# Cross-attention core: the output projection of a tile as one block of twelve matmuls, or as three pieces of four

## The reference

```python
q = (x @ Wq).reshape(b, n, 32, 16)
k, v = jnp.split(ctx @ Wkv, 2, axis=-1)          # 32 heads of 16 each
q = apply_axial_rope(q, pos_map)
k = apply_axial_rope(k, ctx_pos_map)
w = jax.nn.softmax(jnp.einsum('bqhd,bkhd->bhqk', q, k) * scale, axis=-1)
attn = jnp.einsum('bhqk,bkhd->bqhd', w, v).reshape(b, n, 512)
return attn @ Wout + bout                        # x = x + this
```

## Time and profile before

| | us |
|---|---|
| time, median of 3 runs | 2159.01 |
| lowest and highest run | 2152.72 and 2161.05 |
| the profiled execution | 2174.66 |
| its span, first to last instruction | 2172.9 |
| cross core in that span, about | 587 to 1010 |
| mean granted TensorE clock | 0.958 |

### The profile page before, as it was taken

One profiled execution on the slowest core, in us unless ns is written; L12 is line 12 of the kernel. 1 busy time (PEld: TensorE's weight loads), 2 busy tenths in 40 slices (PEclk: granted clock), 3 DMA queues, 4 the chain that ended last, 5 costly groups with the idle time before them and its releaser, 6 DMA issues. The chain is left out here.

```text
span 2172.9 us, 31103 instructions
## 1 busy us (share of the span) xinstructions
PE 2018.2 (93%) x10519; PEld 1340.0 (62%) x10519; DVE 1214.0 (56%) x2649; ACT 873.1 (40%) x1535; POOL 697.4 (32%) x610
## 2 busy tenths in 40 slices
PE   7998999978799999997998899979999998999998
PEld 6875666666433334334776566657878787565664
DVE  6555766566799898875886666644323153222221
ACT  3424444355377676773443444434222221111111
POOL 0003665346423232322664755601000000232332
PEclk9998998989899999997998899989999999999999
DMA  5637676356754646444466767452112055233331
GB/s 199 222 138 187 159 158 140 104 185 250 255 145 118 152 105 154 100 127 128 173 222 205 166 162 160 121 213 105 54 44 78 1 218 208 45 60 60 66 61 36
DMA packets 150832, 297.64 MB, mean 137 GB/s; under 512 B 24594, under 2 KB 43156, under 8 KB 149588
## 3 DMA queue, kind: packets, MB, share of 16 engines
q1 hardware_dynamic: 112900, 242.29, 37.6%
q10 hardware_dynamic: 29040, 34.74, 6.2%
q0 software_dynamic: 8736, 18.62, 4.6%
HBM read 181.55 MB, written 102.50 MB: 131 GB/s over the span
## 5 line engine op out<-in xcount | busy, mean ns | idle before, releaser
L1353 ACT ACTIVATE cross_c_prob<-bank 128x512 f32<-128x512 f32 x512 | 271.1, 598 | 118.9 <-PE bank L1200 117.6
L1402 DVE TENSOR_REDUCE row_max<-bank 128x2 f32<-128x1024 f32 x248 | 290.7, 1213 | 24.6 <-PE bank L1162 23.6
L1860 PE MATMUL bank<-moe_hT,moe_w 128*128 128x512 f32 x1056 | 250.6, 393 | 7.7 <-DVE moe_w L2103 7.7
L1200 PE MATMUL bank<-stack 56*128 56x512 f32 (+4 forms) x768 | 225.7, 437 | 11.9 <-DMA stack<-first_c_max_rows 3.9
L1860 PEld LDWEIGHTS bank<-moe_hT,moe_w 128*128 128x128 f32 x1056 | 199.4, 190 | 50.1 <-issue 7.9
L1162 PE MATMUL bank<-stack 48*128 48x512 f32 (+4 forms) x720 | 184.9, 441 | 26.0 <-PEq L71 13.6
L1200 PEld LDWEIGHTS bank<-stack 56*128 56x128 f32 (+1 forms) x768 | 114.9, 197 | 142.8 <-ACT cross_c_prob L1353 68.5
L1948 PE MATMUL bank<-moe_w_e,moe_hT_e 128*128 x624 | 194.2, 465 | 6.2 <-DMA moe_w_e<-in_experts_packed 5.9
L1948 PEld LDWEIGHTS bank<-moe_w_e,moe_hT_e 128*128 128x128 f32 x624 | 116.4, 191 | 67.3 <-issue 9.6
L1162 PEld LDWEIGHTS bank<-stack 48*128 48x128 f32 (+1 forms) x720 | 92.0, 196 | 101.4 <-DVE row_max L1402 46.1
L1398 DVE CUSTOM_DVE_ANT_0 first_c_masked<-bank,later 128x128 f32<-128x128 f32 (+3 forms) x240 | 110.2, 486 | 75.9 <-PE bank L1162 73.5
(11 more groups left out here) (391 smaller groups left out, 3987.5 us busy)
## 6 DMA issues: line engine op xcount, KB each, us to landing
moe_w_e<-in_experts_packed SPq DMA_DIRECT2D x8, 2176.0 KB, 8.9
qk_parts<-first_p_parts SPq DMA_DIRECT2D x32, 512.0 KB, 2.6
stack<-qk_parts SPq DMA_DIRECT2D x64, 256.0 KB, 7.1
qk_parts<-cross_p_parts SPq DMA_DIRECT2D x32, 512.0 KB, 2.7
stack<-qk_parts SPq DMA_DIRECT2D x256, 64.0 KB, 2.6
qk_parts<-rotary_p_parts SPq DMA_DIRECT2D x32, 512.0 KB, 2.7
moe_raw<-in_shared_packed SPq DMA_DIRECT2D x11, 768.0 KB, 8.4
stack<-qk_parts SPq DMA_DIRECT2D x16, 512.0 KB, 6.3
```

The lines of the kernel that those rows point to most:

```text
L1200: last = nc.tensor.matmul(tiles[:, h], k_stack[slot][r : r + ALL_ROWS, at, m * P : (m + 1) * P], q_stack[slot][r : r + ALL_ROWS, at, q0:S] ...
L1353: nc.scalar.activation(probability(g, m, j), psum[bank_at["score", n]][:, 0:S], ACT.Exp).then_inc(s.exp_done, 1)
L1402: nc.vector.tensor_reduce(row_max[:, g % 2, m, j - 1 : j + 1], c.banks[:, first : first + WIDE, :], AX_X, ALU.max).then_inc(s.max_done, 1)
L1860: last = nc.tensor.matmul(psum[bank][:], weights(pa, f, k), hT[p % 2][:, pb, k, :], start=m == 0, stop=m == len(steps) - 1)
```

## The change

The projection of a tile is issued in three pieces of four matmuls: behind the value blocks of steps 11 and 15 of group `1 + m` and of step 3 of group `2 + m`. `add_residual` follows in DVE's order two steps behind the last piece, at step 5 of group `2 + m`. For the causal cores nothing is different.

```diff
-        THIRDS = 1 if cross else 3
-        OUT_AT = ([[(1 + m, 7)] for m in range(TT)] if cross else
+        THIRDS, RESIDUAL_LAG = 3, 2 if cross else 0
+        OUT_AT = ([[(1 + m, 11), (1 + m, 15), (2 + m, 3)] for m in range(TT)] if cross else
                   [[(1 + m // 2, step) for step in ((12, 14, 15) if m % 2 else (6, 7, 10))] for m in range(TT)])
@@
         def projected_at(g, step):
 
-            if g >= G:
+            if g >= G and step >= 0:
                 for m, thirds in enumerate(OUT_AT):
@@
-                            projected = projected_at(g, step)
+                            projected = projected_at(g, step - RESIDUAL_LAG)
                             if projected and projected[2] == THIRDS - 1:
                                 add_residual(projected[0], projected[1])
```

## The result

The changed kernel takes 2203.96 us (median of 4 runs, 2195.7 to 2210.68), the kernel before 2160.03 in the same comparison (4 runs, 2152.72 to 2167.13). The ratio is 1.0188, 95% interval 1.0166 to 1.0210: slower, by 41 us by the ratio and 44 by the medians; whether by more or less than 2% the interval leaves open. The profiled execution has 2195.7 us and a span of 2194.0.

A forecast was written before the change was run, and what follows sets the result against it. Bounds: PE and ACT waiting for each other in a ring, and DVE equally in quiet groups. Added 1.54 + 1.54 + 2.52 = 5.60 us less 3.58 removed, +2.02 a tile, +24.3 over 12 tiles: 2184 us, range 2168 to 2202.

The forecast's parts named there:

- The block's removal: Projecting groups: the block of twelve matmuls and the transposes' wait for the residual add go, saving 3.58 us a tile.
- pieces behind value blocks: Four projection matmuls each delay the next scoresT pair by their whole length: 1.05 us each, 3.15 for three.
- the hold: Projection's bank held from step 11 to the next group's step 3, leaving two banks: 0.49 us in each of two beats.
- the add on the ring: ScoresT of step 6 waits for maximum and add in series; with its piece, that beat is 2.52 us longer.
- four or more: Rival: gaps at step 6 drop PE's clock, at most 3.45 us each; four falls give 2198, twelve 2225; chance 0.12.
- Faster: Rival: pieces fill PE's waits for exponentials and banks cost nothing; projecting groups 11.52 us, time 2123; chance 0.06.
- behind the scores: PE's slack lies later in the beat, behind the scores; in-order PE cannot use it for pieces put ahead; no size given.
- No difference: Rival: only the pieces cost, 3.15 against 3.58 us a tile, both bank costs vanish; -5 us, 2154; chance 0.05.
- Half: Rival: only one of the hold and the step-6 wait is there, 4.62 us a tile; +12.5 us, 2171; chance 0.12.
- The things costed at nothing: DVE's add, the store on SP, the projection's wait for packing and the residual loads were taken to have no price.

The follow-up runs named there:

- run 3: Against the kernel after, each piece returns its bank at once, pieces not added up, and the add reads residual rows alone, not the bank; 2159.94 us, ratio 1.0000.
- run 1: Against the kernel after, the residual add stands one step behind the last piece, not two; 2169.47 us, ratio 1.0045.
- run 2: Against the kernel after, each piece takes a bank and returns it at once, pieces one and two not added up, the add kept; 2195.33 us, ratio 1.0160.
- run 7: Against the kernel after, the residual add stands four steps behind the last piece, not two; 2231.22 us, ratio 1.0323.
- run 4: Against the kernel after, pieces moved behind the scores of steps 14, 2 and 6, ahead of scoresT, the add at step 6; 2160.68 us, ratio 1.0004.
- run 6: Against the kernel before, the whole block of twelve matmuls stands at step 15, not 7; 2176.17 us, ratio 1.0077.

## Why the prediction was right, and where it was not

**Sign and mechanism held.** The forecast was 2184 us, +1.2%, with 2168 to 2202. The ratio 1.0188 on the 2159.01 that it started from gives 2199.6, near the upper end; the median of the comparison, 2203.96, lies 2 us above it. The block's removal gives 3.58 us a tile; pieces behind value blocks are paid in full; the hold and the add's place come on top. All four were in the working, and the runs separate them:

| a tile, us | predicted | measured |
|---|---|---|
| block and transposes' wait, removed | 3.58 | 3.58 (read from the kernel before, not measured anew) |
| three pieces | 3.15 | 3.45 (run 3) |
| the hold, two beats | 0.98 | 0.95 (run 1 less run 3) |
| the add on the ring | 1.47 | 1.47 (after less run 1) |
| sum added | 5.60 | 5.87 |

The measured sum is 16.78 less 10.91 by construction, as the rows are differences of neighbouring runs. The beat with the third piece is a check by itself. From its value block on, the chain was forecast to reach scoresT pair, scores, maximum, add, the second pair and the next value block at 2.04, 2.37, 2.84, 3.95, 4.79 and 5.12 us; in the timeline after, from 718.73 on, they come at 2.12, 2.46, 2.92, 4.06, 4.80 and 5.23. Over twelve tiles the groups without a drop make +27.5 us, where I had +24.3.

**The pieces were mis-sized.** I took 1.05, bounds 0.99 to 1.10; they have 1.12 (719.73 to 720.85), and the parts around them some hundredths more. (A slip beside it: the upper ends give 2185 by their own sum, not the 2186 that is also written.) My row showed the slow first matmul, 0.34 us, and I left out that the last one ahead of a scoresT pair is slow too (0.32 from the block's last matmul, 703.80, to 704.12). With three pieces both are paid three times.

**The term that failed is the clock.** It stood in the sum at nothing. I set "four or more" drops at 0.12, because the cross core had held 1.00 from 633 to 960 us and only one gap of this length was known to me, in the first core. Six came in the profiled run, 34 us at half clock, 13.7 us of time. That is the larger part of the miss: +24.3 became some +41. The warning was in rows 5, 12 matmuls in 3.4 us and then half clock. The timeline of the kernel before has a gap of 1.86 us there:

```profile
295.63 0.78 PE L1200 MATMUL bank<-stack 104*128 104x512 f32 x1 [1.86 <-DMA stack<-first_c_max_rows]
```

The new gap had 1.8 in my own working. I should have priced it as likely. The Trainium skill (TensorE: Matmul & The Clock Gate, HAM oscillation) tells of a kernel whose waits for DMA, longer than the work between them, drop the clock at every tile. Runs 2 and 7 show the same pattern, a drop for each of twelve tiles, though their waits are for DVE and have only 1.71 and 3.13 us in groups of 17 us and more. The four-drop case had 2198 us, near what was measured, but by luck: it had four drops at 3.45 us each, 13.8 us, and what came was six at 1.3 to 2.8 us each, 13.7 us.

**The rivals.** Faster, by pieces filling holes: run 3 is that case without the banks and is level with the kernel before, and run 4 shows that a better place for the pieces does not help: without the piece's own 1.12 the beat has 2.57 us, against 2.60. My argument against it was right in its result, but the slack "behind the scores" that I named is small, 0.25 us or somewhat more a beat, and the change of kind that a piece brings there uses it up. No difference: this is run 3, 2159.94 us; I had 2154. Half: run 1, with the hold and without the add's wait, 2169.47 us; I had 2171. The things costed at nothing (DVE's add under its cover, the wait for packing, the residual loads) show no wait in the profile. The store on SP was costed at nothing because it stayed ahead of the maxima's sending; run 6 shows what it costs where its add comes late.

**What stays open.** That the gap brings the drops of the projecting part is shown by edits that change the gap and leave PE's order alone (runs 1 and 7, and run 3 against run 2). Why some groups of the kernel after escape with a gap of the same 1.7 us is not settled. Nor is the gap the only way to a drop: at the end of the cross core before, 17.1 us at half clock begin at 981.75 behind pauses of 0.98 us and less, and of the four gaps of 1.2 to 1.4 us in the projecting parts of the two runs with the block at step 11, one was followed by a drop. The split of +41 us into 27.5 and 13.7 comes from one profiled execution; the runs' granted clocks, 0.954 to 0.960, say that others had as much or more.

## What to carry to other kernels

Splitting a block on an in-order engine saves only if the work lands in real idle time; a weight load that waits is room only as far as the engine's own work in the beat, changes of kind included, is shorter than the beat. Before an accumulator is kept open over several steps, walk the bank queue: count how many banks are left, and name the next user of the returned bank and what stands ahead of its release on the other engine. One place in DVE's order was worth 34 of 44 us here. And a new wait on PE can have two prices, as that of 1.7 us had here: its length and the clock behind it.

## What the hardware showed that I had not expected

- A gap of 1.7 us, once a group, was enough to halve PE's clock (2.4 to 1.2 GHz) for 3.4 to 6.8 us in a part of the core that had run at 1.00 throughout. Without the gap (runs 1 and 3) it did so in no projecting group.
- With the same gap of 1.7 us, six stretches came for the twelve tiles of the kernel after, and twelve, one for each tile, in run 2, whose groups are shorter (15.8 against 16.8 us at full clock).
- A change between kinds of matmul is not free: four projection matmuls between a value block and a scoresT pair take 1.12 us, where twelve in a row take 2.97, 0.99 for four.
- Ten stack loads take SP 5.8 us to issue; what is queued behind them is late by as much.
